# Attention and gated low-rank layer on one core: order of the first products with new weights, place of the output sum, places of the gate products

## The reference, cut to what matters

```
xn = layernorm(x)
q = rmsnorm((xn @ Wq.T) per head) * q_norm_w      # 32 heads
k = rmsnorm((xn @ Wk.T) per head) * k_norm_w      # 8 heads
v = xn @ Wv.T
scores = q @ k.T / sqrt(128) + slope[head] * (j - i), masked for j > i
s = concat_heads(softmax(scores) @ v) @ Wo.T
router = 8 * softmax(xn @ Wr.T + br);  low = einsum(xn, A)
g = silu(2 * einsum(low, B, router))
y = x + s * g
```

## Time and profile before

| what | value |
|---|---|
| runs, median of 3 | 746.49 us (745.05 to 747.19) |
| profiled execution | 747.09 us, its span 745.3 us |
| TensorE busy | 97% |
| VectorE busy | 81% |
| ScalarE busy | 75% |
| GpSimd busy | 45% |
| granted TensorE clock | 1.000 of full speed |
| memory traffic | 148.02 MB, 198 GB/s |

### The profile page before, as it was taken

How to read it: one execution, slowest core, us unless ns; L and a number is a source line. 1 busy time by engine, 2 the same in 40 slices (tenths; PEclk the granted TensorE clock), 3 DMA queues, 4 the chain that set the end, 5 groups by cost and what they waited for, 6 DMA issues and landing times.

```text
span 745.3 us, 14609 instructions
## 1 busy us (share of the span) xinstructions
PE 720.7 (97%) x3741; PEld 605.6 (81%) x3741; DVE 600.7 (81%) x1490; ACT 560.5 (75%) x1440; POOL 332.9 (45%) x320
## 2 busy tenths in 40 slices
PE   7999999999999999999999999999999999999997
PEld 6787878878788888888788887888788788888866
DVE  7867898688887889697987889777986879868976
ACT  4566878687877878777876877778787778769972
POOL 4223444354334633644344543437326443445656
PEclk9999999999999999999999999999999999999999
DMA  8015968678695877868686786958677686867761
GB/s 302 2 29 148 276 164 238 194 224 239 162 277 146 227 214 220 233 168 268 165 237 191 221 243 158 286 140 234 202 222 223 177 270 161 242 179 209 202 184 70
DMA packets 214773, 148.02 MB, mean 199 GB/s; under 512 B 48992, under 2 KB 205536, under 8 KB 214624
## 3 DMA queue, kind: packets, MB, share of 16 engines
q1 hardware_dynamic: 184224, 130.39, 60.1%
q10 hardware_dynamic: 30528, 17.38, 9.5%
HBM read 85.84 MB, written 61.87 MB: 198 GB/s over the span
## 4 chain that ended last, share of the span: by engine, by line
PE 52%; DVE 14%; issue 11%; DMA 9%; ACT 6%; POOL 6%; SPq 2%; DVEq 0%; ACTq 0%; POOLq 0%
PE qkv_ps L1364 5%; PE qkv_ps L1365 5%; PE qkv_ps L1366 5%; DMA x_sb<-turning 4%; PE out_ps L1364 4%; PE out_ps L1366 4%; PE out_ps L1365 4%; PE score_ps L1364 4%; PE score_ps L1366 3%; PE score_ps L1365 3%; DVE squared L1039 3%; POOL pt_lo L589 2%; PE mix_ps L1364 2%; PE mix_ps L1366 2%; PE mix_ps L1365 2%
## 5 line engine op out<-in xcount | busy, mean ns | idle before, releaser
L589 POOL TENSOR_TENSOR pt_lo<-x_sb,pt_hi 128x512 fp32r<-128x512 f32 x129 | 164.2, 1295 | 255.4 <-ACT pt_hi L795 255.4
L720 ACT ACTIVATE probs<-probs,neg_max 128x128 f32<-128x128 f32 (+3 forms) x256 | 142.2, 559 | 39.6 <-DVE neg_max L1018 38.3
L1018 DVE CUSTOM_DVE_ANT_0 probs<-score_ps,cst,slope 128x128 f32<-128x128 f32 (+3 forms) x256 | 131.1, 544 | 27.9 <-PE score_ps L1366 27.4
L728 ACT ACTIVATE probs<-probs,recip 128x128 f32<-128x128 f32 (+3 forms) x252 | 126.1, 549 | 8.0 <-DVE recip L1025 8.0
L1364 PE MATMUL qkv_ps<-w_hi,xt_hi 128*128 128x256 f32 (+1 forms) x392 | 126.0, 321 | 3.1 <-DVE xt_lo L961 1.7
L1365 PE MATMUL qkv_ps<-w_lo,xt_hi 128*128 128x256 f32 (+1 forms) x392 | 125.7, 321 | 0.0
L1366 PE MATMUL qkv_ps<-w_hi,xt_lo 128*128 128x256 f32 (+1 forms) x392 | 125.2, 319 | 0.0
L795 ACT ACTIVATE pt_hi<-x_sb 128x512 fp32r<-128x512 f32 x153 | 86.6, 624 | 48.3 <-issue 31.1
L1364 PE MATMUL out_ps<-wo_hi,o_hi 128*128 128x512 f32 x252 | 102.5, 407 | 2.2 <-DVE o_lo L1063 1.9
L1039 DVE STREAM_TRANSPOSE squared<-probs 128x256 f32<-128x256 f32 (+3 forms) x124 | 101.8, 822 | 0.3 <-ACT probs L728 0.3
L579 POOL TENSOR_TENSOR inv_rms<-sums,minus_half 128x5 f32<-128x5 f32 x64 | 76.4, 1193 | 57.5 <-DVE sums L1077 57.5
(11 more groups left out here) (191 smaller groups left out, 1589.9 us busy)
## 6 DMA issues: line engine op xcount, KB each, us to landing
qk_moved<-turning_qk SPq DMA_DIRECT2D x60, 320.0 KB, 3.4
turning_qk<-qk_squared ACTq DMA_DIRECT2D x212, 80.0 KB, 2.0
turning<-squared SPq DMA_DIRECT2D x120, 128.0 KB, 2.4
x_sb<-turning SPq DMA_DIRECT2D x30, 512.0 KB, 4.9
w_raw<-wqkv SPq DMA_DIRECT2D x32, 384.0 KB, 5.3
turning<-squared SPq DMA_DIRECT2D x120, 96.0 KB, 2.0
x_sb<-turning SPq DMA_DIRECT2D x30, 384.0 KB, 4.3
turning<-squared SPq DMA_DIRECT2D x128, 64.0 KB, 1.8
```

The lines of the kernel that those rows point to most:

```text
L589: nc.gpsimd.tensor_tensor(by_quad(pt_lo, j), moved_block(t, j), by_quad(pt_hi, j).bitcast(F32), ALU.subtract).then_inc(pt_lo_by_pool, 1)
L720: nc.scalar.activation(probs[:, h, 0:n], probs[:, h, 0:n], ACT.Exp, bias=neg_max[:, h:h + 1], scale=-1.0, accum_out=total[:, h:h + 1]).the ...
L728: nc.scalar.activation(to[:, h, 0:n], probs[:, h, 0:n], ACT.Copy, scale=recip[:, h:h + 1]).then_inc(probs_ready, 1)
L1018: nc.vector.tensor_tensor_reduce(probs[:, h, 0:n], score_bank(t, h), cst[:, C_DIST + SEQ - n:C_DIST + SEQ], slope[:, h:h + 1], HUGE, ALU.a ...
```

## The change

For the first unit with new weights, TensorE makes the products that need w_hi alone first (xt_hi and xt_lo by w_hi, for q and then for k and v), and then, chunk by chunk, the products with w_lo, q and k with v alternating. It now waits for w_hi_done in the first pass. VectorE's add_out stands behind turned_qk_lo (in w_slot also behind the second square_probs). In the last group gate_tangents of blocks 0 and 1 stand ahead of the probabilities in slot 3; the gate products of blocks 0 and 1 move to slot 3, those of 2 and 3 to slot 4, those of 4 and 5 to where 2 and 3 were, and those of 6 and 7 behind mixed_lo of the last block but one.

```diff
--- before.py
+++ after.py
@@ -813,14 +813,14 @@
                     split_w(g + 1, range(0, EARLY_W + 1))
                 if here(t, left):
                     exponentials(g, t, range(0, HPG))
+                if left == 1 and t == 3:
+                    gate_tangents(range(0, 2))
                 if w_due:
                     split_w(g + 1, range(EARLY_W + 1, KC))
                 if left == 1 and t == W_SLOT:
                     turned_qk_hi(g, t + 1)
                 if here(t, left):
                     normalize_probs(g, t, range(0, 2))
-                if left == 1 and t == 3:
-                    gate_tangents(range(0, 2))
                 if left == 1 and t == 4:
                     gate_tangents(range(2, 6))
                 if here(t + 1, left) and not (left == 1 and t == W_SLOT):
@@ -1159,10 +1159,10 @@
                 split_w(g + 1, range(W_DVE - 1, W_DVE))
                 normalize_q(g, t + 2)
                 square_both(g, t + 2)
-                add_out(g, t - 3)
                 square_probs(g, t, 0)
                 turned_qk_lo(g, t + 1)
                 square_probs(g, t, 2)
+                add_out(g, t - 3)
                 set_factor(g, t + 3)
 
             def last_w_slot(g, t):
@@ -1210,8 +1210,8 @@
                     value_lo(g, t + 2)
                 if here(t, left):
                     reciprocals(g, t, 0)
-                if left == 1 and t == 4:
-                    multiply_gate(range(0, 2))
+                if left == 1 and t in (3, 4):
+                    multiply_gate(range(2 * (t - 3), 2 * (t - 3) + 2))
                 if here(t + 2, left):
                     normalize_k(g, t + 2)
                 if here(t, left):
@@ -1219,12 +1219,12 @@
                 if here(t + 2, left):
                     normalize_q(g, t + 2)
                     square_both(g, t + 2)
-                if here(t - 3, left):
-                    add_out(g, t - 3)
                 if here(t, left):
                     square_probs(g, t, 0)
                 if here(t + 1, left):
                     turned_qk_lo(g, t + 1)
+                if here(t - 3, left):
+                    add_out(g, t - 3)
                 if here(t - 2, left) and not wide(t + 1):
                     mixed_lo(g, t - 2, left)
                 if here(t, left):
@@ -1240,7 +1240,7 @@
                 reciprocals(g, before, 0)
                 bias(g, before, 3, singly=True)
                 add_out(g, before - 3)
-                multiply_gate(range(2, 4))
+                multiply_gate(range(4, 6))
                 mixed_lo(g, before - 2, 1)
                 reciprocals(g, before, 2)
                 for h in range(3):
@@ -1252,10 +1252,9 @@
                 for n in range(keys_of(before)):
                     turned_lo(before, n)
                 reciprocals(g, last, 2)
-                multiply_gate(range(4, 6))
                 add_out(g, before - 1)
+                mixed_lo(g, before, 1)
                 multiply_gate(range(6, BLOCKS))
-                mixed_lo(g, before, 1)
                 for n in range(keys_of(last)):
                     turned_lo(last, n)
                 last_y(before, 0, out_ps[:, :], slice(0, DM))
@@ -1403,6 +1402,30 @@
                 if c == KC - 1:
                     last.then_inc(kv_ready, 1)
 
+            def project_new(g, t):
+
+                m = t % BLOCKS
+                rows = slice(m * P, (m + 1) * P)
+                parts = ((q_ps(t), slice(0, QW)), (qkv_ps[:, 1, 0:QKV - QW], slice(QW, QKV)))
+                for k, (to, cols) in enumerate(parts):
+                    if k == 1:
+                        pe.wait_ge(k_norm_ready, ONE(g, t - 1, 1))
+                        pe.wait_ge(v_lo_ready, ONE(g, t - 1, 1))
+                    for c in range(KC):
+                        if k == 0:
+                            pe.wait_ge(w_hi_done, (g + t // BLOCKS) * KC + (c + 1))
+                        pe.matmul(to, xt_hi[:, c, rows], w_hi[:, c, cols], start=c == 0, stop=False)
+                        pe.matmul(to, xt_lo[:, c, rows], w_hi[:, c, cols], start=False, stop=False)
+                for c in range(KC):
+                    if c < W_DVE:
+                        pe.wait_ge(w_lo_by_dve, (g + t // BLOCKS - 1) * W_DVE + (c + 1))
+                    else:
+                        pe.wait_ge(w_lo_by_pool, (g + t // BLOCKS - 1) * (KC - W_DVE) + (c - W_DVE + 1))
+                    for (to, cols), done in zip(parts, (q_ready, kv_ready)):
+                        last = pe.matmul(to, xt_hi[:, c, rows], w_lo[:, c, cols], start=False, stop=c == KC - 1)
+                        if c == KC - 1:
+                            last.then_inc(done, 1)
+
             def project(g, t, chunks=range(KC)):
 
                 if two_banks(t) and t % BLOCKS > 0:
@@ -1411,13 +1434,7 @@
                     for c in chunks:
                         project_kv(g, t, c)
                 elif two_banks(t):
-                    for c in range(EARLY_W):
-                        project_q(g, t, c)
-                    for c in range(EARLY_W):
-                        project_kv(g, t, c)
-                    for c in range(EARLY_W, KC):
-                        project_q(g, t, c)
-                        project_kv(g, t, c)
+                    project_new(g, t)
                 else:
                     for c in chunks:
                         project_q(g, t, c)
```

## The result

The changed kernel takes **739.85 us** (median of 9 runs, 738.81 to 743.20) against 747.19 us (745.05 to 753.17, 9 runs on the same chip): ratio 0.9902, 95% interval 0.9875 to 0.9928. That is 7.3 us less (5.4 to 9.3 by the interval). Faster was forecast, but by 4.1 us only, and the median lies 1.05 us under the range's low end of 740.9. The profiled execution took 743.02 us with a span of 741.2 us. It is one of the two longest of its nine, so its span alone (4.1 us less than before) would have seemed to confirm the forecast.

What follows compares the result with a forecast made beforehand. TensorE, busy 720.7 of 745.3 us, was taken as the bound, so only its waits counted, k_lo's ending last. Span 745.3 - 3.3 - 1.2 + 0.4 = 741.2, by the median 742.4 us; range 740.9 to 745.4.

Steps and rivals of the forecast that it cites:

- Part 1: Slot 5's projection, w_hi products first: 0.6 us a group by itself, worth nothing while k_lo comes no sooner.
- The new wait for w_hi: Slot 5's projection would wait for the fourth w_hi, which ScalarE makes behind the exponentials; at most 0.88 us in the latest group.
- Part 2, slot 5: add_out behind q_lo and k_lo makes k_lo 0.58 us sooner in seven groups: 3.3 us saved, bounds 0 and 4.0.
- late first bias: After slot 5, VectorE's full queue makes the next scores' first bias late: 0.09 us lost a group, leaving 0.49 of 0.58.
- Part 2, block 2: Scores before block 2 wait for k_lo three times of eight; 0.4 us each saves 1.2 us, bounds 0 and 1.7.
- Part 2, where it can cost: Slots 0 and 4: VectorE idles before q_lo, later work 0.39 us late; taken as 0, 5.9 us if nothing covers it.
- Part 3: Gates and tangents placed anew in the last group: +1.3 us in slots 3 and 4, -0.7 and -0.2 at the end, +0.4.
- rival 3: Gate products in slots 3 and 4 and GpSimd operations block each other in full, chain 2.2 us late: 744.2 us, chance 0.12.
- the earlier writes: First pair of probabilities turned 0.58 us earlier, so SyncE starts its writes earlier; counted as nothing, bounds -0.5 and 0.
- 1 (half comes back): Rival: the saved time returns at TensorE's next wait, half of the 4.5 us left: 744.6 us, chance 0.19.
- 2 by k_lo's distance: Rival: k_lo is bound from elsewhere (ScalarE's k_hi), moving add_out gains nothing: 746.9 us, chance 0.06.
- 4 by slots 0 and 4: Rival: VectorE stands at q_lo in slots 0 and 4, 0.39 us reaching the scores each time: 748.3 us, chance 0.06.

Runs made afterwards that it cites:

- gates_only: Kernel before with only the last group's gate products and tangents at their new places: 747.87 us, ratio 1.0010.
- runs of the halves: Kernel before with add_out moved behind q_lo and k_lo in slot 5 alone (745.08 us, 0.9968), and in all slots but slot 5 (745.94 us, 0.9976).
- sum_only: Kernel before with only add_out moved behind q_lo and k_lo in all slots, old product order and gates: 741.33 us, ratio 0.9917.
- sum_ahead_lo_first: Changed kernel with, in w_slot, add_out ahead of the first reciprocals and q_lo and k_lo ahead of both squares of the probabilities: 741.12 us, ratio 0.9927.
- lo_before_squares: Changed kernel with q_lo and k_lo ahead of both squares of the probabilities in w_slot: 750.73 us, ratio 1.0032.

## Why the prediction was right and wrong

In short: the mechanism was right, a sum that nobody waits for stood in front of the value that releases TensorE. What failed is the size of three terms, slot 5 (3.3 us, by the traces 4.1), the waits before block 2 (1.2, by the traces 1.9) and the gates (+0.4, by the traces -0.6), and a range whose low end left out that the terms' own bounds could be met together.

**Part 1, right.** The order alone is worth nothing (1.0011), and w_lo's waits turned into k_lo's. With the sum moved it shortens the chain by 0.19 us and gives 0.13 back, 0.4 us in seven groups. The new wait for w_hi was 0.19 to 1.3 us, in four groups, beyond the 0.88 that I called the most; the distance was 4.22 in that group too, so it cost nothing.

**Part 2, slot 5: right mechanism, 0.8 us too small.** k_lo comes 0.60 us sooner, forecast 0.58, and still ends last. Two deductions were wrong. The 0.09 us for a late first bias came out as 0.02: slot 6 took 10.07 us before and takes 10.09. And the seventh group, for which I took 0.4, gained the full 0.60. So 7 x (0.60 - 0.02) = 4.1 us in place of 3.3.

**Part 2, block 2: too small.** Forecast 1.2 us from three waits of 0.4. The three were a draw: waits before block 2 come when a transfer lands late, in 16 of 28 groups, which is four of seven. And each is worth 0.5: in the trace of before k_lo delays the three starts by 0.37 to 0.39 us, and the refill of 0.10, which the prediction had inside its 0.4, comes on top in slot 2. Slot 1 gives 7 x 0.20 = 1.4 us (± 0.5), slot 2 another 7 x 0.07 = 0.5. Together 1.9 us, above the bound of 1.7. That is the step that was most in error for its size among those that save.

**Part 2, where it can cost: right.** VectorE's idle time in front of q_lo rose from 1.5 us in 2 waits to 4.8 in 10, and slots 0 and 4 kept their lengths.

**Part 3, wrong in sign by the traces.** Forecast +0.4. Timelines of the last group, before (what the earlier trace rows left out of GpSimd):

```profile
684.05 1.16 POOL L579 TENSOR_TENSOR inv_rms<-sums,minus_half 128x5 f32<-128x5 f32 x1
...
685.28 0.20 POOL L583 TENSOR_TENSOR inv<-inv_rms,factor 128x5 f32<-128x5 f32 x1
...
693.79 1.61 POOL L579 TENSOR_TENSOR inv_rms<-sums,minus_half 128x5 f32<-128x5 f32 x1
```

and after:

```profile
680.80 1.16 POOL L579 TENSOR_TENSOR inv_rms<-sums,minus_half 128x5 f32<-128x5 f32 x1
...
681.36 1.29 DVE L1132 SCALAR_TENSOR_TENSOR gate<-wo_raw,gate 128x512 f32<-128x512 f32 x2 [1.16 <-ACT wo_raw L713]
682.03 0.67 POOL L583 TENSOR_TENSOR inv<-inv_rms,factor 128x5 f32<-128x5 f32 x1
682.74 0.29 DVE L1088 TENSOR_TENSOR squares<-qkv_ps,inv 128x128 f32<-128x128 f32 x1
...
691.02 1.18 POOL L579 TENSOR_TENSOR inv_rms<-sums,minus_half 128x5 f32<-128x5 f32 x1
...
693.20 0.28 DVE L1088 TENSOR_TENSOR squares<-qkv_ps,inv 128x128 f32<-128x128 f32 x1
```

The pair took 1.29 us beside GpSimd, where I had let it take up to 1.82. That 1.82 of the earlier trace rows I had misread as 0.3 us on each product: taken singly, the first took 1.22 us (693.16 to 694.38) and the second 0.68. The first ended 0.55 us behind GpSimd's last product on the probabilities (pt_lo, until 693.83), so it was held in full, and by that plain product, not by the power operation of rival 3. GpSimd's power operation starts 682.74 - 680.80 = 1.94 us ahead of VectorE's next step, where it was 685.51 - 684.05 = 1.46; so the chain is 0.5 late and not 0.9. In slot 4 the same distance is 693.20 - 691.02 = 2.18 against 695.71 - 693.79 = 1.92, 0.3 and not 0.4. TensorE sees 0.5 us in these two slots (21.71 to 22.24). The end brought 1.1 us, forecast 0.9: over all traces the stretch from slot 5 of the last group to the end took 44.0 to 44.7 us with the gates moved and 45.0 to 45.9 without, 44.4 and 45.5 in the mean. VectorE hardly waits for GpSimd any more. But the forecast had the two terms the wrong way round. GpSimd's rows, before and then after:

```profile
729.43 1.60 POOL L599 TENSOR_TENSOR acc<-acc,w_raw 128x512 f32<-128x512 f32 x1
730.99 1.72 POOL L597 TENSOR_TENSOR acc<-acc,gate 128x512 f32<-128x512 f32 x1
```

```profile
727.72 1.62 POOL L599 TENSOR_TENSOR acc<-acc,w_raw 128x512 f32<-128x512 f32 x1
729.98 1.29 POOL L606 TENSOR_TENSOR acc<-acc,gate 128x512 f32<-128x512 f32 x1 [0.64 <-DVE gate L1132]
...
732.67 0.69 DVE L1145 TENSOR_TENSOR acc<-out_ps,gate 128x512 f32<-128x512 f32 x1 [0.38 <-POOL wo_raw L608]
```

The gap of 0.68 in front of 727.73 is gone, but a new one of 0.64 stands in front of 729.98, as the last gates are now made later. What came back is the 0.2 us that I had called an estimate: beside VectorE's gates three of GpSimd's operations took 1.60 to 1.72 us before (the two rows, and the 1.62 of the earlier trace rows) and one takes 1.62 now, against 1.29 alone; that is 0.7 us. So 0.5 - 1.1 = -0.6 us by the traces; gates_only, at +0.7 us with 1.5 to either side, can't tell it from nothing nor from the forecast.

**The sum.** -4.1 - 1.9 - 0.6 = -6.6 us by what the traces now give, against a measured -7.3 (-9.3 to -5.4) and a forecast of -4.1. It is inside the interval; the remaining 0.7 us isn't attributed. Two things can hold it, and the runs don't separate them. The kernel before was 746.49 us in the three runs from which I forecast and 747.19 in nine, 0.7 us of scatter; 746.49 - 6.6 is 739.9, and 739.85 was measured. And the earlier writes, which I counted as nothing with a bound of -0.5, are worth 1.0 ± 0.9 us by the traces. The runs of the halves agree with the traces: 7 x (0.41 + 0.11) = 3.6 us of slot 5 against 2.4 ± 1.6, and 1.9 of the other slots against 1.8 ± 2.1. **The range** failed by its own rule: the lower bounds of the terms, -4.0, -1.7 and -1.2, add up to -6.9 or 739.6 us. I set its low end at 740.9, as if they could not be met together. The rivals fall: 1 (half comes back) by sum_only, 2 by k_lo's distance, 3 by the pair of 1.29 us, 4 by slots 0 and 4.

## What to carry to other kernels

Work that nobody is waiting for belongs behind the values that release the bottleneck engine, and one such move can be worth more than the wait view of one trace shows: here it also made later transfers harmless in slots that looked free in the trace read. Count with each wait the refill behind it. Before moving an instruction further ahead, look at what the other engines do in its new place: here q_lo lost 0.51 us beside GpSimd's w_lo. Where a wait depends on a transfer that scatters, count the slots in which it can happen, not those in which it did. A range must reach as far as the terms' own bounds added up.

## What the runs showed of the hardware

**The turned probabilities land with a scatter of some 2 us.** Measured from the scores of block 3, ScalarE's move behind that transfer starts 22.4 to 24.1 us later in most groups (24.7 at most), though the last of its two reads is issued at 17.2 to 17.6 in most. As the fourth w_hi follows mostly 6.3 us behind it, slot 5 lasts 11.2 to 13.4 us in the one execution of the changed kernel that the trace shows. The Trainium skill, "DMA: Bandwidth & Descriptors", section "Latency and other measured facts", gives the latency of HBM as 0.2 us on average and 2 us at high load; the spread here is of that size, but no run here separates it from the waiting of the queues.

**VectorE and GpSimd lengthen each other's plain products.** In slot 3 the pair took 1.29 us beside the power operation, which itself took 1.16 as before; but GpSimd's small product behind it took 0.67 us instead of 0.20, and ended at 682.70, just behind the pair at 682.65. For a plain product the lock that the prediction cited ("SBUF — State Buffer" of the Trainium skill, section "Who interferes with whom") fits, with GpSimd as the one that waits there and VectorE in sum_ahead_lo_first, where q_lo takes 1.16 us and ends 0.55 behind GpSimd's w_lo, as the first gate product of the earlier trace rows ends 0.55 behind pt_lo. With the power operation it depended on which came first: begun 0.56 us ahead of the pair (680.80) neither lost time, but begun inside the pair, at 693.79 in the trace of before (the pair from 693.16 to 694.98), it took 1.61 us in place of 1.16.

**The start-up has a clock of its own.** Windows of the start, TensorE's granted clock in the third column from the right, before, after, and in lo_before_squares:

```profile
0.00:20.00 20.00, 15.10 (x90) 13.32 (x91) 14.82 (x36) 8.59 (x17) 9.63 (x14) 1.00 0.78 283
```

```profile
0.00:20.00 20.00, 15.97 (x87) 14.19 (x88) 14.15 (x36) 7.85 (x12) 9.03 (x14) 0.91 0.76 282
```

```profile
0.00:20.00 20.00, 15.23 (x79) 13.93 (x79) 13.83 (x26) 7.52 (x12) 8.57 (x12) 0.83 0.76 282
```

In windows of 1 us the lower level is seen: after has 0.50 to 0.52 from 8 to 11 us (0.50 is the 1.2 GHz level, 1.00 the 2.4 GHz one), behind a microsecond without products (7 to 8), and lo_before_squares 0.50 from 9 to 14; but before has such a microsecond too (7 to 8) and kept 1.00. From 20 to 730 us it is 1.00 in all three. The first scores of the main loop start at 61.80, 62.52 and 64.99 us. The clock isn't all of it: over the fourteen traces they start at 61.2 to 62.8 us with 1.00 in the first 20 us, at 62.5 to 64.1 with 0.91. The start-up's code is the same in all these kernels, so 3 to 4 us of difference between two single executions can come from there; of a change of 4 us that must be known before spans are subtracted.
